# Performer block on one core: the keys pass folds its sums in another PSUM bank, and ScalarE instead of VectorE writes a constant table

## What is computed

```python
q, k, v = (einsum('bsd,dhk->bhsk', xn, w) for w in (wq, wk, wv))      # 16 heads of 32
def phi(u):                                                           # 128 features
    proj = einsum('bhsk,mk->bhsm', u, omega)
    return exp(proj - 0.5*sum(u*u) - max(proj)) / sqrt(128) + 1e-6
pq, pk = phi(q * s), phi(k * s)
kv, z = einsum('bhsm,bhsk->bhmk', pk, v), sum(pk, axis=2)             # over a batch's 1024 rows
h = (einsum('bhsm,bhmk->bhsk', pq, kv) / einsum('bhsm,bhm->bhs', pq, z)) @ wo
y = layernorm(xn + h); y = layernorm(y + gelu(y @ w1 + b1) @ w2 + b2)
r = sigmoid(xr @ W_r.T) * (relu(xk @ W_k.T)**2 @ W_v.T)               # xr, xk: mixes of xn and the row before
out = x + y + r
```

## Time and profile before

| | |
|---|---|
| median of 3 runs | 3503.1 us (3502.72 to 3503.34) |
| the profiled execution's own time | 3506.75 us |
| its span, first to last instruction | 3505.0 us |
| PE busy | 3429.3 us (98%) |
| PEld busy | 3155.7 us (90%) |
| DVE busy | 2469.8 us (70%) |
| ACT busy | 1969.5 us (56%) |
| POOL busy | 1104.0 us (31%) |
| mean granted PE clock | 0.992 of full |

### The profile page before, as it was taken

The page is one execution under the profiler, slowest core; times in us unless marked ns, Lnnn a source line. Parts: engine busy times, 40 slices in busy tenths (PEclk is TensorE's granted clock), DMA queues, the critical chain, the costliest instruction groups (busy, mean ns, idle before and its releaser), DMA issues.

```text
span 3505.0 us, 77429 instructions
## 1 busy us (share of the span) xinstructions
PE 3429.3 (98%) x29993; PEld 3155.7 (90%) x29993; DVE 2469.8 (70%) x4840; ACT 1969.5 (56%) x4239; POOL 1104.0 (31%) x861
## 2 busy tenths in 40 slices
PE   7999999999899999999999999999999999999998
PEld 6888888888788888888888889999999999999998
DVE  5776777776767777777777766666666666666666
ACT  6777777777565666666666654444444444444443
POOL 3555444544445555554545533000000000000000
PEclk9999999999899999999999999999999999999999
DMA  3222222222323233333232346444444444444443
GB/s 122 79 83 73 83 83 82 76 76 75 95 84 108 92 114 105 102 107 112 90 116 90 112 130 217 145 148 147 149 147 145 145 147 148 145 145 145 145 145 126
DMA packets 195355, 409.83 MB, mean 117 GB/s; under 512 B 27440, under 2 KB 52528, under 8 KB 194992
## 3 DMA queue, kind: packets, MB, share of 16 engines
q1 hardware_dynamic: 194992, 404.89, 34.3%
HBM read 292.50 MB, written 112.33 MB: 116 GB/s over the span
## 4 chain that ended last, share of the span: by engine, by line
PE 70%; DVE 2%; ACT 1%; issue 0%; DMA 0%; POOL 0%; ACTq 0%; POOLq 0%; DVEq 0%
PE ffn_hidden L175 30%; PE attend_gated L175 19%; PE ffn_result L175 8%; PE attend_num L175 6%; PE attend_feat L1416 3%; PE attend_feat L1436 1%; PE ffn_turn L1901 1%; PE attend_turn L1406 1%; DVE attend_kvz_lo L1384 1%; DVE attend_pT_lo L1345 1%; PE attend_feat L1443 1%; PE attend_turn L1425 0%; ACT attend_kvz_hi L1290 0%; DVE attend_kvz_lo L1387 0%; DMA ffn_r_in<-in_L_attn_w_dram 0%
## 5 line engine op out<-in xcount | busy, mean ns | idle before, releaser
L175 PE MATMUL ffn_hidden<-ffn_yT_hi,ffn_wa_hi 128*128 128x256 f32 x2048 | 574.5, 281 | 4.1 <-DVE ffn_wa_lo L1789 2.4
L175 PE MATMUL ffn_hidden<-ffn_yT_lo,ffn_wa_hi 128*128 128x256 f32 x2048 | 573.7, 280 | 0.0
L175 PE MATMUL ffn_hidden<-ffn_yT_hi,ffn_wa_lo 128*128 128x256 f32 x2048 | 572.5, 280 | 0.0
L311 POOL TENSOR_TENSOR ffn_n_rstd<-ffn_n_base,ffn_n_power 128x2 f32<-128x2 f32 x32 | 27.5, 859 | 1299.8 <-DVE ffn_n_negmean L306 1299.8
L1771 ACT ACTIVATE ffn_ht_hi<-ffn_hs 128x512 fp32r<-128x512 f32 x248 | 156.3, 630 | 426.2 <-DVE ffn_hs L1818 426.2
L175 PEld LDWEIGHTS ffn_hidden<-ffn_yT_hi,ffn_wa_hi 128*128 128x128 f32 x2048 | 385.4, 188 | 4.7 <-DVE ffn_wa_lo L1789 2.6
L175 PEld LDWEIGHTS ffn_hidden<-ffn_yT_hi,ffn_wa_lo 128*128 128x128 f32 x2048 | 385.6, 188 | 0.0
L175 PEld LDWEIGHTS ffn_hidden<-ffn_yT_lo,ffn_wa_hi 128*128 128x128 f32 x2048 | 385.2, 188 | 0.2
L627 POOL TENSOR_TENSOR keys_z_sum<-keys_z_sum,keys_e 128x512 f32<-128x512 f32 x192 | 259.7, 1371 | 233.4 <-ACT keys_e L695 233.4
L1822 DVE TENSOR_TENSOR ffn_ht_lo<-ffn_hs,ffn_ht_hi 128x512 fp32r<-128x512 f32 x248 | 173.5, 700 | 218.7 <-ACT ffn_ht_hi L1771 218.7
L1756 ACT ACTIVATE ffn_hid<-ffn_hidden,ffn_bias 128x256 f32<-128x256 f32 x496 | 205.7, 467 | 179.4 <-PE ffn_hidden L175 179.4
(11 more groups left out here) (296 smaller groups left out, 11678.5 us busy)
## 6 DMA issues: line engine op xcount, KB each, us to landing
ffn_tq<-part_d SPq DMA_DIRECT2D x248, 512.0 KB, 4.1
keys_xin<-in_L_attn_x_dram SPq DMA_DIRECT2D x32, 512.0 KB, 4.5
xn_d<-keys_xn SPq DMA_DIRECT2D x32, 512.0 KB, 3.0
xT_d<-keys_xT_whole SPq DMA_DIRECT2D x32, 512.0 KB, 2.6
u_d<-keys_uq SPq DMA_DIRECT2D x32, 512.0 KB, 3.1
shared_xTf<-xT_d SPq DMA_DIRECT2D x32, 512.0 KB, 5.7
shared_uq<-u_d SPq DMA_DIRECT2D x32, 512.0 KB, 4.8
r_d<-shared_gate SPq DMA_DIRECT2D x32, 512.0 KB, 3.2
```

The costliest lines, as they stand in the source:

```text
L175: last = pe.matmul(out, stationary[a], moving[b], start=start and n == 0, stop=stop and n == len(TERMS) - 1)
```

## The change

- The fold goes to bank `ring0` instead of `turn`, except in the last three groups. Its PE wait becomes `kv_added` (DVE has added the last `kv` part of the group, the previous content of ring0) instead of `k_split`. `turn_x` half 0 no longer waits for `fold_out`; the first `kv` part, which writes ring0 next, does.
- In the first group alone, the second half of `turn_x` uses ring0, so that PE doesn't wait for DVE to have read the first half.
- `pick` is written by ACT, ahead of its first squares, and no longer by DVE.

```diff
@@ -182,6 +182,11 @@
+def by_half(bank):
+
+    return bank[:, :].rearrange("p (a n) -> p a n", a=2)
@@ -478,7 +483,10 @@
         def fold_bank(g, c):
-            return feat[c].t if g == G - 1 else turn
+            return feat[c].t if g == G - 1 else turn if g >= G - 3 else ring[0]
+
+        def turn_of(g, n):
+            return ring[0] if g == 0 and n == 1 else turn
@@ -662,7 +670,7 @@
-                    act.activation(xT[i % 2].hi[:, 2 * n:2 * n + 2, :], turn_halves, ACT.Copy).then_inc(xT_hi, 1)
+                    act.activation(xT[i % 2].hi[:, 2 * n:2 * n + 2, :], by_half(turn_of(g, n)), ACT.Copy).then_inc(xT_hi, 1)
@@ -743,7 +751,7 @@
-                    dve.tensor_tensor(xT[i % 2].lo[:, 2 * n:2 * n + 2, :], turn_halves,
+                    dve.tensor_tensor(xT[i % 2].lo[:, 2 * n:2 * n + 2, :], by_half(turn_of(g, n)),
@@ -822,12 +830,11 @@
                     if n == 0:
                         wait(pe, k_split, 2 * g)
-                        wait(pe, fold_out, pieces_before(g - 2))
-                    else:
+                    elif g > 0:
                         pe.wait_ge(x_split, 2 * g + 1)
                     for c in range(2):
                         for t in range(TG):
-                            last = pe.transpose(turn[:, c * GT + t * P:c * GT + (t + 1) * P],
+                            last = pe.transpose(turn_of(g, n)[:, c * GT + t * P:c * GT + (t + 1) * P],
@@ -882,6 +889,7 @@
                     elif n == 0:
                         pe.wait_ge(kv_added, NC * g)
+                        wait(pe, fold_out, pieces_before(min(g, G - 3)))
@@ -904,7 +912,9 @@
-                    if g < G - 1:
+                    if g < G - 3:
+                        pe.wait_ge(kv_added, NC * g + NC)
+                    elif g < G - 1:
                         pe.wait_ge(k_split, min(2 * g + 6, 2 * G))
@@ -1289,13 +1299,12 @@
+            act.wait_ge(mask_made, 2 * HC + 1)
+            act.activation(pick[:, :, :], mask[:, :].unsqueeze(2).broadcast_to([P, NC, M]), ACT.Copy).then_inc(pick_ready, 1)
             run(act, do, ACT_BODY)
             return do
 
         def vector(dve):
-            dve.wait_ge(mask_made, 2 * HC + 1)
-            dve.tensor_copy(pick[:, :, :], mask[:, :].unsqueeze(2).broadcast_to([P, NC, M])).then_inc(pick_ready, 1)
-
```

## The result

| | before | with the change |
|---|---|---|
| median, of 4 runs each | 3503.22 us (3502.72 to 3504.45) | 3482.31 us (3480.15 to 3487.89) |
| ratio | | 0.9938 (95% interval 0.9926 to 0.9949) |
| the profiled execution's own time | 3506.75 us | 3484.01 us |
| its span | 3505.0 us | 3482.2 us |
| PE busy | 3429.3 us | 3422.0 us |

The account below looks back on a forecast made before the run. PE was taken to set the pace in the keys loop, the fold's wait its one hole. 16.5 + 1.7 + 3.9 = 22.1 us less, from 3503.1 to 3481.0 us; range 3476.5 to 3488.5.

Parts of the forecast that it names:

- The fold: 16.5 expected: Keys loop: without the transposes' 26 waits for ACT's copy of the fold, 16.5 us less.
- the ends 12.1 and 17.1: Keys loop: bounds in us, from PE's matmul row and from idle weight loads plus the transposes' restart.
- The half closed hole: Rival, keys loop: PE meets `turn_x` half 1 too early, half of 16.5 lost; gain 13.9, 3489.2 us; chance 0.13.
- the cover of 0.9 us: Keys loop: time between the end of DVE's split and the earlier start of `turn_x` half 1; the thinnest cover.
- The slower rival: Keys loop: `kv`'s new wait for the fold's copy holds up PE, 1.1 us each time; 3510 us; chance 0.02.
- its point of decision, 2.7 us: Keys loop: `kv`'s new wait decides once ACT's copy of the fold ends over 2.7 us later.
- That the loop was paced by DVE: Rival, keys loop: the 26 waits are hidden, only 5.6 us left from the other places; 3497.5 us; chance 0.03.
- The first half: 1.7 expected: First 18 us: the first group's second transposes and first projection come 1.7 us earlier, between 0.9 and 2.6.
- `pick`: 3.9 expected: Start of the attend pass: `top` 2.5 us earlier plus 1.4 from the clock; bounds 6.5 and -0.8.
- the lower bound of 0.8: Start of the attend pass: if POOL's clearing holds the mix until 942.8, 0.8 of the 2.5 us is left.
- the clock's share: Start of the attend pass: PE's lower clock falls again but for shorter; 1.4 us, between 0 and 4.0.
- the first rival's middle: Slow end of the range, given as 3488.5, for the half closed hole in the keys loop; chance 0.13.

Follow-up runs that it names:

- e1: The kernel before with only the fold moved to ring0 with its waits; 3489.71 us, ratio 0.9959.
- e4: The changed kernel with ACT's copy of the fold moved behind the second half of `v_out`, in the loop only; 3514.66 us, ratio 1.0026.
- e6: The changed kernel with POOL clearing by four subtractions that read SBUF in place of two memsets; 3486.63 us, measured once.
- e5: The changed kernel with `pick` back on DVE and POOL's two clearings moved behind its first mix lo part; 3483.49 us, ratio 0.9939.
- e3: The kernel before with only `pick` moved to ACT; 3502.17 us, ratio 0.9992.
- e2: The kernel before with only the first group's second half of `turn_x` in ring0; 3503.16 us, ratio 0.9994.
- e7: The changed kernel with ACT's `pick` moved behind both squares and the mix copy, to its first k job; 3479.46 us, ratio 0.9925.
- e10: The changed kernel with the late `pick` of e7 and the late clearing of e5 together; 3477.77 us, ratio 0.992.
- e8: The changed kernel as it is, timed again; 3484.06 us, ratio 0.9936.
- e9: The changed kernel with the late `pick` of e7, timed again beside the change; 3480.2 us, ratio 0.9926.

## Why the prediction was right, step by step

It gave 3481.0 us; 3482.31 were measured, so the gain was 20.9 instead of 22.1 us.

**The fold: 16.5 expected, 16.5 measured.** The loop is 16.51 us shorter in the change and 16.57 in e1. The choice between the ends 12.1 and 17.1 was the step that mattered. PE's wait row counts 0.47 us a fold; the idle weight loads and the spacing of starts give 0.63, and 26 x 0.63 = 16.4 is what came. In the windows PE's idle time fell only by 12.5 us, so the other 4 us had been counted as PE's busy time; that they were the last matmul's tail is my reading and not measured by itself. e4 shows the same in the other direction, 0.91 by the row and 1.17 by the length.

**The rivals of the loop.** The half closed hole didn't come about: DVE's split stayed where it was behind the fold, as that rival said, and the cover of 0.9 us measured 0.92 in the fold shown. It was used up in none of the 26 bodies: PE's one wait for `xT_lo` at the transposes stands in the head. It is the next thing that a faster PE meets. The slower rival's mechanism is real (e4), and its point of decision, 2.7 us, was right (2.6 in e4); the change stays inside it because ACT is idle ahead of the copy, then as now. That the loop was paced by DVE is excluded by e1. My "under 2" for the idle time in the fold stretch was wrong, 3.1: I had not looked at what lay in the last groups of the kernel before, where 3.5 us of idle (880 to 906 us) had nothing to do with the fold.

**The first half: 1.7 expected, 1.74 at the place.** What arrives at the end hangs on the clock. Without the lower clock the head takes 47.58 us without the edit (e1) and 46.03, 45.92 and 45.82 with it (the change, e6, e4): 1.6 to 1.8 less. Where it is granted as briefly as before, 48.15 (e5) against 49.89 and 49.90 (before, e3): 1.7 less. But in e2 and e7 to e10 the lower clock lasts about twice as long, and the head is only 0.2 to 0.6 us shorter. Whether the edit makes that longer stretch likelier stays open; three profiles without the edit (before, e1, e3) aren't enough to say, nor is it known what part the chip has that ran them. One sentence of the prediction fails here: that PE's wait of 1.7 us ahead of 43.2 "was enough" for the lower clock. The same wait, 1.67 us, stands in the change at 39.45, and no lower clock follows.

**`pick`: 3.9 expected, 3.0 in the profiled pair.** Each step to `top` came within 0.1 us of the one worked out: ACT's `pick` 0.63, `top` 2.4 us earlier. The mix wasn't held. This was where the Trainium skill (SBUF — State Buffer, "Who interferes with whom") was weighed, which says that only a GpSimd operation that reads SBUF holds up a DVE operation with two SBUF inputs, and any GpSimd operation a DVE copy or cast in a two-port mode. Both halves agree with these runs: mix 1.67 us beside memsets and 6.62 beside reading operations, cast 3.72 beside memsets and 0.43 without. That the cast ran in a two-port mode is in no row. The total can't decide it: with the lower bound of 0.8 for the step the sum would have been 20.4, or 19.0 with no share of the clock, and both lie within the interval of 17.9 to 25.9.

The mis-sized term was the clock's share, 1.4 expected. As forecast, the clock fell again at the second features, for less time: from about 927.7 to 934.5 us, where before it was 947.8 to 958.0. But from the fourth bank on (927.53 and 950.01), which is where PE no longer waits for `top`, the lower clock lasts 6.8 us against 8.0, and that part is 10.56 us long against 11.10: 0.5 less. With the 2.4 of the wait this is the 3.0 of the place. The pair that begins at the lower clock gives 3.4 (e2 and e8). So the place was put 0.5 to 0.9 too high.

**What is due to luck.** Of the profiled pair's 22.8 us, the loop gives 16.5, the attend start 3.0 and the head 3.9, of which over 2 us are the lower clock that happened to stay away (the first transposes, 0.3 us later, take some of it back). The medians' 20.9 has no profile of its own, so how much of this is in it isn't known. That it lies 1.2 us from 22.1 is closer than an interval of 8 us can promise; the loop's 16.5 is the part that was really hit. The range had two slips. Its fast end was taken from 26.6, where the bounds add up to 26.2, so it should have been 3476.9; and its slow end is called the first rival's middle but stands at 3488.5, where that rival gives 3489.2. Neither touches the result.

**Where the gain could still be had.** My account of `pick` let ACT wait nearly 3 us for the mask and said that this "costs only what DVE's `sq` waits". That was the sentence to stop at: the change leaves the mask in front of `top`, as the kernel before did, and `top` doesn't need it. e7 and e9 take that away. Against the change timed beside them that is 3.9 us more (e9 to e8), which the stretch shows too (19.56 to 15.68); the intervals of the two ratios still overlap. PE has no wait there any more, and the mean granted clock of the stretch is 0.74 where the change had 0.68 and 0.71.

## What to carry to other kernels

Price a removed wait by the spacing of the starts around it, or by the idle weight loads, not by the matmul row's own wait: here 0.63 against 0.47 us, times 26. When a wait is moved from one instruction to a later one, work out the cover at the new place and of the next thing queued behind it; here both numbers, 2.7 and 0.9 us, held to a tenth. And when a slow constant is in the way, first ask what makes it slow and who needs it: the cast was slow because of its neighbour on POOL, and the best of the places tried was behind everything that was urgent.

## What the runs showed that I had not expected

- A 128x4 copy on DVE took 3.14 us beside POOL's two memsets (e7, e9) and 0.17 us otherwise (e10). In e9 it starts 0.43 us after the first memset and ends at 926.40, when the second does (924.57 + 1.80, by e9's rows of POOL): the smallest copy was held for the whole series.
- The lower clock near 43 us comes in some executions only, and not for one length: none in e1, e4, e6 and one profile of the change, about 3.4 us before and in e3 and e5, about 6.8 us in e2 and e7 to e10. The head of one and the same program differs by 3.6 us with it (46.03 and 49.66). The five profiles with the long stretch are also the five whose attend start begins at the lower clock.
- The first transposes start between 11.76 (e5) and 12.88 us (e10) with nothing edited ahead of them; a comparison of two profiles from zero carries that difference along.
